# Transformer layer on 8 cores: the feed-forward stage's output stores moved behind the next segment's first loads in SyncE's queue

## The reference

```python
x = x + attn(layernorm(x), Wq, Wk, Wv, Wfc)   # x: [4, 8192, 1024] f32
# feed-forward, on x2 = layernorm(x):
gate = einsum('bsd,hd->bsh', x2, w_gate / 127)   # 1024 -> 3072
up   = einsum('bsd,hd->bsh', x2, w_up / 127)     # 1024 -> 3072
h    = silu(gate) * up
x    = x + einsum('bsh,dh->bsd', h, w_down / 127)  # 3072 -> 1024
```

## Time and profile before

| | us |
|---|---|
| median of 2 runs | 3755.62 (3751.20 and 3760.03) |
| the profiled execution, its own time | 3748.07 |
| its span on the slowest core (core 4) | 3746.5 |
| spans of the 8 cores | 3724.1 to 3746.5 |
| median span of die 0 / die 1 | 3729.1 / 3737.5 |

### The profile page before, as it was taken

The page is one execution under the profiler, slowest core; times in us unless marked ns, Lnnn a source line. Parts: engine busy times, 40 slices in busy tenths (PEclk is TensorE's granted clock), DMA queues, the critical chain, the costliest instruction groups (busy, mean ns, idle before and its releaser), DMA issues. The chain is left out here.

```text
span 3746.5 us, 38294 instructions; the slowest of 8 cores (3724.1 to 3746.5 us)
## 1 busy us (share of the span) xinstructions
PE 2292.7 (61%) x12192; PEld 1171.6 (31%) x12352; DVE 1937.8 (52%) x2305; ACT 683.0 (18%) x1691; POOL 1124.1 (30%) x447
## 2 busy tenths in 40 slices
PE   4333444455565555655545543587878869797887
PEld 2111112232333333333333332233333324333333
DVE  5433459987887877878778787111111111111111
ACT  0122231222222221222222211210111101011110
POOL 1000004644635546455464456210110101010100
PEclk9999986677766776667767666699999989899999
DMA  6446310000001000010010000254444445344444
GB/s 99 125 152 201 113 54 1 23 12 23 23 23 34 12 23 23 23 34 12 23 33 13 23 6 12 74 159 133 151 141 141 153 145 163 121 163 130 146 148 141
DMA packets 109631, 302.39 MB, mean 81 GB/s; under 512 B 13184, under 2 KB 29568, under 8 KB 108416
## 3 DMA queue, kind: packets, MB, share of 16 engines
q1 hardware_dynamic: 68736, 159.41, 13.6%
q0 software_dynamic: 32640, 121.65, 10.6%
q10 hardware_dynamic: 8064, 18.88, 1.3%
HBM read 247.46 MB, written 60.82 MB: 82 GB/s over the span
## 5 line engine op out<-in xcount | busy, mean ns | idle before, releaser
L563 POOL TENSOR_TENSOR avB<-Aa,Vs 128x4096 bf16<-128x4096 bf16 x128 | 957.0, 7496 | 1065.4 <-PE pOT L588 733.5
L588 PE MATMUL pOT<-ident,avB 128*128 128x128 bf16 x4096 | 350.2, 266 | 332.9 <-POOL avB L563 332.9
L833 DVE TENSOR_TENSOR hseg<-sg,pU 128x512 bf16<-128x512 bf16 x192 | 132.0, 688 | 703.6 <-PE pU L828 703.6
L814 PE MATMUL pG<-x2s,wgS 128*128 128x512 bf16 x1505 | 372.8, 389 | 122.1 <-DMA wgS<-d_wgT 119.8
L588 PEld LDWEIGHTS pOT<-ident,avB 128*128 128x128 bf16 x4096 | 333.4, 122 | 352.8 <-issue 346.7
L828 PE MATMUL pU<-x2s,wuS 128*128 128x512 bf16 x1505 | 367.2, 385 | 20.1 <-DMA wuS<-d_wuT 18.3
L856 PE MATMUL pD<-hseg,wdC 128*128 128x512 bf16 x1501 | 350.5, 388 | 17.3 <-DMA wdC<-d_wdT 13.8
L270 PE MATMUL wps<-ident,wstg_b 128*128 128x128 bf16 x832 | 187.1, 264 | 284.2 <-ACT wstg_b L249 133.4
L803 POOL DMA_DIRECT2D wuS<-d_wuT x192 | 103.0, 537 | 806.7 <-PE pU L828 747.8
L478 DVE TENSOR_TENSOR gramB<-Qs,Ks 128x4096 bf16<-128x4096 bf16 x128 | 319.7, 2498 | 25.9 <-ACT Vs L466 12.6
L490 DVE TENSOR_TENSOR gh<-gramB 128x2048 bf16<-128x2048 bf16 x128 | 303.0, 2368 | 13.7 <-DVE gramB L478 0.5
(11 more groups left out here) (78 smaller groups left out, 2071.9 us busy)
## 6 DMA issues: line engine op xcount, KB each, us to landing
wuS<-d_wuT POOLq DMA_DIRECT2D x192, 256.0 KB, 3.1
wgS<-d_wgT SPq DMA_DIRECT2D x192, 256.0 KB, 2.7
wdC<-d_wdT POOLq DMA_DIRECT2D x64, 768.0 KB, 4.6
xcT<-x SPq DMA_DIRECT2D x32, 512.0 KB, 5.0
d_x<-x1p SPq DMA_DIRECT2D x32, 512.0 KB, 3.8
x1s<-d_x SPq DMA_DIRECT2D x8, 2048.0 KB, 14.9
y<-yst SPq DMA_DIRECT2D x32, 512.0 KB, 4.2
wstg_i<-wg SPq DMA_DIRECT2D x24, 512.0 KB, 3.6
```

What stands on the lines that cost most here:

```text
L563: e.tensor_tensor(avB[g % 2][:].rearrange("p (t h d) -> p t h d", t=4, d=64), bass.AP(Aa[e4][:].tensor, Aa[e4][:].offset + 64 * g, [[256, ...
L588: e.matmul(pOT[:, 128 * b:128 * (b + 1)], avB[g % 2][:, 1024 * i + 128 * b: 1024 * i + 128 * (b + 1)], ident[:], start=(g == 0 and i == 0 ...
L814: e.matmul(pG[h % 2][:], wgS[h % 2][:, j * 128:(j + 1) * 128], x2buf[xp][j][:], start=(j == 0), stop=(j == 7)),
L833: lambda e, h=h: e.tensor_mul(hseg[h][:], sg[h % 2][:], pU[h % 2][:]),
```

## The change

The four stores of yst are no longer put into SP's queue at the end of their segment. They are kept in a list (y_pend) and put in during the next segment's gate pass, after everything of block h = 1 and before wgS of block h = 2. Their own wait (all 32 additions of their segment) and their count on dy are the same. So SP's order at the turn becomes: x1s, the eight x2 slices of the next segment, wgS(0), wgS(1), the four y stores, wgS(2). The stores of the last segment are put in after the loop. The other engines' orders, all waits and all buffers are as before.

```diff
             S = Sched(cnt, hwm)
+            y_pend = []
             for s8 in range(8):
...
                           inc="dmul")
+                    if h == 1:
+                        for fn in y_pend:
+                            fn()
+                        y_pend = []
                 S.add("sync",
...
                 for tb in range(4):
-                    S.add("sync",
-                          lambda e, s8=s8, tb=tb:
-                          e.dma_start(y_out[s8 * 512 + tb * 128:
-                                            s8 * 512 + (tb + 1) * 128, :],
-                                      yst[tb][:]),
-                          waits=[("dadd", 32 * (s8 + 1))], inc="dy", incn=16)
+                    def mk(s8=s8, tb=tb):
+                        def emit():
+                            S.add("sync",
+                                  lambda e, s8=s8, tb=tb:
+                                  e.dma_start(y_out[s8 * 512 + tb * 128:
+                                                    s8 * 512 + (tb + 1) * 128, :],
+                                              yst[tb][:]),
+                                  waits=[("dadd", 32 * (s8 + 1))],
+                                  inc="dy", incn=16)
+                        return emit
+                    y_pend.append(mk())
+            for fn in y_pend:
+                fn()
             S.add("sync", lambda e: e.nop(), waits=[("dy", 64 * 8)])
```

## The result

The changed kernel takes 3664.02 us (median of all 11 executions) against 3754.24 us before (median of 10): the ratio is 0.9754, 95% interval 0.974 to 0.9767, so 92 us of 3754 are gone. The ratios, and the times of all kernels from here on, leave out executions in which one die ran at a lower granted clock than the other (3 of these 11; the other eight have a median of 3663 us). The profiled execution took 3656.86 us, 91 less than that of before (3748.07); its slowest core is core 7, span 3655.3.

The account below looks back on a forecast made before the run. The feed-forward stage was taken to be bound by TensorE, its span shrinking one for one with TensorE's idle time. 94 + 15 - 14 - 0 = 95 us off 3748 gave 3653 us, range 3635 to 3691.

Parts of the forecast that it names:

- The wait, 94 us: At seven segment turns, TensorE's idle wait for the first gate tile, about 13.4 us each, goes: 94 us gained.
- Rival C: At the turn, SP held by its full queue or GpSimd's tiles gating keep the wait: 3748 us, chance 0.05.
- few us: Behind x1s, the many short x2 issues hold SP a few us, with nothing due on it for 70.
- The clock after the wait, 15 us: First gate matmuls after each turn no longer run at the lower clock: 2.2 us times seven, 15 us gained.
- The y stores, 14 us paid: In the next gate pass, y traffic makes wgS(2) land late: 2.0 us times seven, 14 us lost, bounds 0 and 20.
- the neighbour in the queue sets the landing: At the turn, wgS(2) right behind y in SP's queue lands like the x2 slice formerly there, after 5.9 us.
- The loads in the phase change, nothing: At the down pass's start, x2 slices and wgS(0) moved beside x1s and wdC cost nothing; 0 to 32 us open.
- rival B: Traffic of moved loads and y gives much of the gain back: 57 us saved, 3691 us, chance 0.11.
- Rival D: In the dense passes, TensorE without its seven rests is granted a lower clock: slower, 3864 us at 0.82; chance 0.05.

Follow-up runs that it names:

- e1: Kernel before the change, with only the next segment's eight x2 slices put ahead of the four y stores in SP's queue; ratio to before 0.9899.
- e2: Kernel before the change, with the y stores at their old place but issued from ScalarE's queue instead of SP's; ratio to before 0.9749, 3663 us.
- e10: Kernel with late transposes, four buffers and early loads, plus a segment's last four transposes behind the next segment's first up matmuls, y behind h = 5; 3549 us.
- e3: Changed kernel with the y stores of the first seven segments left out and nothing in their place; ratio to before 0.9712, 3649 us.
- e5: Changed kernel with the next segment's x2 slices issued one per block at h = 8 to 15, instead of all behind x1s; ratio to before 0.9748.
- e7: Changed kernel with four buffers instead of two for each of wgS and wuS, and y stores behind h = 3; 3620 and 3615 us.
- e8: Changed kernel with transposes one down block late, four wgS and wuS buffers, y behind h = 3, and x1s, x2 and first two wdC loads moved earlier; 3550.21 us.
- e4: Changed kernel with the y stores behind h = 5 instead of h = 1; ratio to before 0.9846.
- e9: Changed kernel with the y stores behind h = 0 instead of h = 1; ratio to before 0.9886, two executions, 3701 and 3741 us.
- e6: Changed kernel with each down block's four transposes issued behind the next block's 24 matmuls instead of ahead of them; ratio to before 0.9565.

## Why the prediction was right, step by step

**The wait, 94 us: right.** The rest fell from 13.70 to 0.37 us, 13.33 a turn, 93.3 us in seven. e1 and e2 show the mechanism: the line in SP's queue. Rival C, that the loads don't come early, falls with it. SP was held longer than the "few us" of the prediction, 11.36 us in the longest case (segment 1), but wgS(0) was out at 2666, over 60 us before its use:

```profile
2654.06 0.59 SPq L845 DMA_DIRECT2D x1s<-d_x  x1
2654.69 11.36 SPq L794 DMA_DIRECT2D x2s<-d_xn2T  x8
```

**The clock after the wait, 15 us: mis-sized.** G(0) to G(1) gave back 1.34 us a turn (5.79 to 4.45), 9 us in all. The step that failed is "the short gaps of 1 to 3 us inside the passes leave the clock at 1.00 and 0.97, and after the change the turn holds no longer one". The turn did hold none longer than 1 us, and still 33 of 56 turns have matmuls at half rate. Before, it was all 56. The premise was read from one segment of one core; over all eight cores of before, 38 stretches of low clock begin in this stage away from the turns. e10 shows that the low clock at the turn goes when the rest for the last transposes goes.

**The y stores, 14 us paid: right in size where the clock is full, too much in the mean.** G(1) to G(2) grew by 0.97 us a turn, 7 us in all. The two terms are not independent. In the 33 turns of the changed kernel with a slow G(0), G(1) to G(2) takes 3.72 us; in the 23 with a full clock it takes 5.49, 2.0 over 3.45, which is the stall that I took. Both kinds need the same 8.9 us from G(0) to G(2): a slow G(0) only spends the time for which wgS(2) would be waited for anyway. The timeline of the sixth turn of core 7 shows the second kind:

```profile
3346.40 1.89 PE L815 MATMUL pG<-x2s,wgS 128*128 128x512 bf16 x8 [1.52 <-DMA wgS<-d_wgT]
```

So 15 - 14 was forecast and 9 - 7 measured; the errors cancel because they are one effect. I had sized the two terms apart and did not see this, so that their sum came out is luck. I was wrong to think that the neighbour in the queue sets the landing: e2 has y on another queue and the same stall, and e3 without y has none.

**The loads in the phase change, nothing: right.** G(22) to D(2) went from 26.68 to 26.85 us, 1 us in seven segments. e5 takes the slices away from there and gains nothing, so rival B falls. The slices do stand behind x1s: issued at 2655 us they land after 15.7 us instead of 3 to 6, and nothing needs them. The DMA issues of the changed kernel on core 7 from 2655 us (KB each, us to landing):

```profile
wdC<-d_wdT POOLq DMA_DIRECT2D x2, 768.0 KB, 12.6
x2s<-d_xn2T SPq DMA_DIRECT2D x3, 128.0 KB, 15.7
```

This is as the Trainium skill has it (DMA: Bandwidth & Descriptors, Queues, rings and completion order): a queue is consumed in order. Over the stage x1s lands in 14.1 us in the median, and was 14.9 before.

**The rest.** 0.3 us a segment more in G(4) to G(22), 2 us in all. 93 + 9 - 7 - 1 - 2 = 92 us, against a forecast of 95.

**Rival D, the clock, did not decide here but is real.** The profiles of before and after have no 0.81 in this stage. In the kernels with fewer waits it is there: e7 and e8 were granted 0.81 for up to 122 and 170 us of the stage on some cores, and e8's cores of die 1 end 21 us later in the median than those of die 0. The Trainium skill (TensorE: Matmul & The Clock Gate, Seeing it yourself) tells of a limit of 13/16 that takes a whole die when three of its cores run dense matmuls, and holds while the load lasts. The trace has its figure, 0.81, but not the rest: in e7 cores 0 and 1 had it for 122 us and cores 2 and 3 of the same die never, and it came in stretches of 5 to 15 us. That it follows from density is not shown. The kernels also differ in DMA traffic at one time, and e4 and e9, with no denser matmuls than the changed kernel, had 0.81 for 5 to 20 us. And all six experiments with 0.81 (e4, e6 to e10) ran on one chip, all four without it (e1, e2, e3, e5) on another; none of them was profiled on both.

## What to carry over

A store that waits for the last result of a phase must not stand ahead of the next phase's loads in an in-order queue; move the loads ahead, or the store to another queue, which was worth the same here. Where the store then runs matters as much: at a moment when the next tiles are already in their buffers it cost 1.5 us here, in the steady pass with two buffers 6.5, and one tile short 7.3. And two costs that meet at one place, a slow clock and a late tile, cost the longer of them here, not their sum.

## What the hardware showed that I had not expected

- In 33 of 56 turns of the changed kernel the clock was at its lower level in the 4 us from G(0) on, behind rests of 1.0 and 0.4 us around four small transposes. Without them it was not (e10, 0 of 56). Behind the same rests between the down blocks D(2) to D(7) a low stretch began in 4 of 384.
- y stores on another queue delay wgS(2) as much as in its own (4.39 and 4.45 us from G(1) to G(2)).
- A granted clock of 0.81, on pairs of cores (0 and 1, 4 and 5, and so on) at the same times, while others keep 1.00: for 95 to 175 us on the pairs that had it in the densest kernels (e7, e8, e10; 619 us on cores 2 and 3 of e10), mostly in stretches of 5 to 8 us (15 on cores 0 and 1 of e7), and for 5 to 20 us in e4, e6 and e9. Before and after do not have it.
